# A Perceiver block on one core: in the blocks that project V, the previous head's value products between the two halves of the scores

## What is computed

```python
q = (layernorm(x) @ Wq + bq).reshape(B, L, NKV, G, HDIM)      # 8 kv heads, 4 query heads each
k, v = split(ctx @ Wkv + bkv)                                 # 6272 keys, 8 heads of 128
scores = einsum("blkgd,bmkd->bkglm", q, k) / sqrt(128)
attn = softmax(scores, axis=-1)
o = einsum("bkglm,bmkd->blkgd", attn, v)
x = x + o @ Wo + bo
...
w = NF4[codes] * scales          # 4-bit weights of the second part, expanded ahead of use
```

## Time and profile before

| | |
|---|---|
| median of 3 runs | 1162.08 us (1157.77 to 1168.44) |
| the profiled execution | 1156.21 us |
| its span, first to last instruction | 1154.40 us (mean granted TensorE clock 0.968) |
| block 0 starts, block 55 starts | 67.08 us, 1032.40 us |
| PE, DVE, POOL, ACT busy | 94%, 82%, 54%, 39% of the span |

### The profile page before, as it was taken

How to read it: one execution, slowest core, us unless ns; L and a number is a source line. 1 busy time by engine, 2 the same in 40 slices (tenths; PEclk the granted TensorE clock), 3 DMA queues, 4 the chain that set the end, 5 groups by cost and what they waited for, 6 DMA issues and landing times. The chain is left out here.

```text
span 1154.4 us, 23709 instructions
## 1 busy us (share of the span) xinstructions
PE 1079.8 (94%) x7035; PEld 954.4 (83%) x7035; DVE 945.8 (82%) x2331; ACT 444.6 (39%) x993; POOL 627.0 (54%) x1303
## 2 busy tenths in 40 slices
PE   6889999999999999899999999999999999995587
PEld 4889989899899989799899889998999999982132
DVE  3358998889988889888899888999898998884365
ACT  2134444344443444334443434444434443431030
POOL 2036675665666666656656666657666556652100
PEclk9689999999999999999999999999999999996879
DMA  9512121112212122121221221212221111114991
GB/s 358 201 38 70 57 63 59 60 53 71 59 47 72 55 61 62 53 59 51 65 63 51 64 65 50 70 41 62 72 63 49 56 43 51 47 46 161 337 379 55
DMA packets 66852, 99.26 MB, mean 86 GB/s; under 512 B 7780, under 2 KB 34916, under 8 KB 65956
## 3 DMA queue, kind: packets, MB, share of 16 engines
q1 hardware_dynamic: 63954, 86.97, 23.9%
q10 hardware_dynamic: 2178, 8.34, 2.1%
q0 software_dynamic: 592, 2.40, 0.6%
HBM read 82.79 MB, written 14.89 MB: 85 GB/s over the span
## 5 line engine op out<-in xcount | busy, mean ns | idle before, releaser
L439 POOL TENSOR_SCALAR leaf<-bit 128x256 f32<-128x256 uint16 x896 | 402.4, 449 | 113.0 <-DVE bit L776 29.1
L788 DVE COPY_PREDICATED leaf<-bit,leaf 128x256 f32<-128x256 uint16 x784 | 388.4, 541 | 50.4 <-POOL leaf L439 14.6
L461 POOL TENSOR_TENSOR leaf<-leaf,scale 128x256 f32<-128x256 f32 x112 | 81.2, 735 | 185.3 <-DVE leaf L788 184.4
L644 ACT ACTIVATE v_hi<-p_kv 128x256 fp32r<-128x256 f32 x196 | 75.2, 384 | 175.6 <-PE p_kv L61 175.5
L59 PE MATMUL p_kv<-wkv_hi,ctx_even_hi 128*128 128x256 f32 x448 | 128.1, 286 | 5.6 <-DVE v_lo L727 4.6
L644 ACT ACTIVATE k_hi<-p_kv,bk_sb 128x448 fp32r<-128x448 f32 x112 | 70.8, 632 | 156.6 <-PE p_kv L61 156.1
L739 DVE TENSOR_TENSOR pt_lo<-p_t,pt_hi 128x512 fp32r<-128x512 f32 x224 | 128.8, 611 | 1.6 <-ACT pt_hi L655 1.2
L655 ACT ACTIVATE pt_hi<-p_t 128x512 fp32r<-128x512 f32 x224 | 115.0, 542 | 33.9 <-PE p_t L544 33.8
L60 PE MATMUL p_kv<-wkv_lo,ctx_even_hi 128*128 128x256 f32 x448 | 125.9, 281 | 0.0
L61 PE MATMUL p_kv<-wkv_hi,ctx_even_lo 128*128 128x256 f32 x448 | 125.7, 281 | 0.0
L727 DVE TENSOR_TENSOR v_lo<-p_kv,v_hi 128x256 fp32r<-128x256 f32 x196 | 82.2, 419 | 46.0 <-ACT v_hi L644 45.6
(11 more groups left out here) (190 smaller groups left out, 2523.7 us busy)
## 6 DMA issues: line engine op xcount, KB each, us to landing
code<-in_codes SPq DMA_DIRECT2D x56, 256.0 KB, 2.6
scale<-in_scales SPq DMA_DIRECT2D x112, 128.0 KB, 3.0
expanded_weights<-leaf SPq DMA_DIRECT2D x112, 128.0 KB, 1.7
wring<-expanded_weights SPq DMA_DIRECT2D x28, 512.0 KB, 12.5
ctx_st<-in_ctx_t SPq DMA_DIRECT2D x96, 112.0 KB, 2.1
wq_sb<-in_wq SPq DMA_DIRECT2D x8, 1024.0 KB, 14.0
wring<-in_wo SPq DMA_DIRECT2D x16, 512.0 KB, 12.4
stage<-in_wkv ACTq DMA_DIRECT2D x4, 1024.0 KB, 8.6
```

The costliest lines, as they stand in the source:

```text
L439: m = nc.gpsimd.tensor_scalar(leaf[:, b, slot, :], bit0[:, b * HW:(b + 1) * HW], NF4[2 * j + 1] - NF4[2 * j], NF4[2 * j], ALU.mult, ALU.add)
L461: nc.gpsimd.tensor_tensor(leaf[:, b, 4, :], leaf[:, b, 0, :], scale[:, b * HW:(b + 1) * HW], ALU.mult).then_inc(scaled, 1)
L644: nc.scalar.activation(dst, src, ACT.Identity, bias=0.0 if bias is None else bias).then_inc(kv_rounded, 1)
L788: return nc.vector.copy_predicated(leaf[:, b, slot, :], bit[:, b * HW:(b + 1) * HW], leaf[:, b, other, :])
```

## The change

On PE, `scores` takes the list of halves that it is to compute. In even blocks the order becomes half 0 of the scores, `prev_values`, half 1 of the scores, `values`. Odd blocks stay as they are. On DVE, in even blocks, `add_output` of block i-2 and three takes of the weight expansion (`high_by_bit2(i-1, 0)` and the two of `high_by_bit1(i-1, 1)`) move from behind `score_stats` to between its two halves. No instruction is added or taken away, and no buffer changes.

```diff
-            def scores(i, h, kuse, static):
-                for c in range(2):
+            def scores(i, h, kuse, static, halves):
+                for c in halves:
                     pe.wait_ge(kv_split, kuse + c + 1)
...
-                scores(i, h, kuse, first)
-                if not first:
-                    prev_values(s, h)
                 if h % 2 == 0:
+                    scores(i, h, kuse, first, (0,))
+                    if not first:
+                        prev_values(s, h)
+                    scores(i, h, kuse, first, (1,))
                     values(s, h, half)
+                else:
+                    scores(i, h, kuse, first, (0, 1))
+                    if not first:
+                        prev_values(s, h)
...
-            def score_stats(i, h, half):
+            def score_stats(i, h, half, meanwhile=None):
                 now = 0 if half else 3
                 for c in range(2):
+                    if c == 1 and meanwhile:
+                        meanwhile()
                     for r in range(RT):
...
-                score_stats(i, h, half)
-                if not (first and h < 2):
+                def finish_previous():
+                    add_output(i - 2, (h - 2) % NKV)
+                    high_by_bit2(i - 1, 0)
+                    high_by_bit1(i - 1, 1)
+
+                score_stats(i, h, half, finish_previous if h % 2 == 0 and not (first and h == 0) else None)
+                if h % 2 == 1 and not (first and h < 2):
                     add_output(i - 2, (h - 2) % NKV)
                 if h % 2 == 0:
                     if not (first and h == 0):
-                        high_by_bit2(i - 1, 0)
-                        high_by_bit1(i - 1, 1)
                         high_by_bit2(i - 1, 1)
```

## The result

The changed kernel takes 1210.94 us (median of 4 runs, 1208.58 to 1219.25), the kernel before 1163.35 beside it: ratio 1.042, 95% interval 1.035 to 1.049. It is slower by 4.2%, where 1210 us was forecast. The profiled execution took 1210.41 us, its span 1208.6.

What follows compares the result with a forecast made beforehand. PE's order was taken to bound the kernel, DVE close behind. 17 x 1.95 + 9 x 1.72 + 0.98 = 49.7 us on the profiled 1156.21 made 1205.9, or 1211.8 by the median; 1210 was given, range 1190 to 1226.

Steps and rivals of the forecast that it cites:

- The wait for `pt_lo`: PE, even blocks, ahead of the value products: a new wait of 0.87 us, plus 0.10 restart, 0.97 in all.
- The wait ahead of V: PE, even blocks, half 1's score reads before V: a new wait of 0.88 us, plus 0.10 restart, 0.98 in all.
- The moved work on DVE: DVE, even blocks, between the score halves: addition and three takes cost nothing, DVE being free half a microsecond early.
- No catch-up: V's stalls (0.53, 0.28) and the odd block's 0.42 us come again unchanged, shifted with V: a gain of nothing.
- The 17 blocks: Even blocks like the one shown, paying both new waits: 1.95 us each, 33.2 us together.
- The 9: Even blocks where `pt_lo` ends 1.90 us after the block's start instead of 2.13: 1.72 us each, 15.5 together.
- The one behind the loop's turn: One even block where DVE has caught up, so only the second wait is paid: 0.98 us.
- The level: Base for the sum: profiled execution 1156.21 us gives 1205.9; the median, 5.9 above, gives 1211.8.
- Rival 1: DVE's catch-up shrinks the old stalls and pays part back: 20 us less, 1190 us; chance 0.11.
- rival 2: DVE sets the period, `pt_lo` ends 0.9 us earlier, no first wait: 15 us faster, about 1147; chance 0.03.
- Rival 3: Moved takes run at 0.73 us instead of 0.37, too late for half 1: 13 us more, 1223; chance 0.08.
- Rival 4: PE's clock falls to 1.2 GHz, twelve scores cost 2.0 us more, 27 times: 54 us, 1264; chance 0.04.

Runs made afterwards that it cites:

- The run with the tile's own wait: Changed kernel, but V's tile 0 waits only for the first score read of half 1, tile 1 for the second: 1200.86 us, ratio to before 1.037.
- the short takes: Takes cut to 8 of 256 columns, table values made small: kernel before 1114.08 us, ratio 0.959; changed kernel 1162.22 us, ratio 1.000.
- the two moved stalls: Two runs on the kernel before: odd blocks' value products split around half 1, 1158.98 us; `v_lo` of tile 4 made ahead of a take, 1162.30 us.

## Why the prediction was right

- **The wait for `pt_lo`** was put at 0.87 us; 0.84 was measured in the block shown, with the release at 0.05 (587.67 to 587.72) and the restart at 0.10 (587.72 to 587.94 instead of 0.12) as in rows 6.
- **The wait ahead of V** was put at 0.88 and measured at 0.88. Every piece of it came from before: the latency from a score matmul to its read, though seen only once, at the loop's turn, held.
- **The even block** was to grow by 1.95 us and grew by 24.58 - 22.72 = 1.86. The missing 0.09 is small change: `pt_lo` ended 2.08 us into this block (2.13 in the one of rows 4 and 5), and half 1's six starts span 591.36 - 590.33 = 1.03, not 1.06.
- **The moved work on DVE** cost nothing, as said, with 0.84 us to spare and not 0.5.
- **No catch-up.** The predicted zero was right: the odd block and V's inner stall came back unchanged. The reason given (everything hangs on V's start) was nearly right. The run with the tile's own wait shows that it hangs on the first `v_lo`, which follows V's start only as long as ACT is free.
- **The sum**, 49.7 us, met 49.5 us in the loop, partly by luck. The 17 blocks grew by 33.1 us, where 33.2 was forecast. The 9 grew by 16.3 and not 15.5. The one behind the loop's turn was to grow by 0.98 and became 0.26 shorter: it pays the second wait only, as said, but the granted clock stayed at 1.00 there, where the kernel before had 0.50. The odd blocks and the first one bring another 0.4. So the excess of the 9 and the gift of the clock cancel.
- **A cover that the prediction missed.** In three of the 9 blocks (the first of a chunk, inside the loop), the 0.05 us from `pt_lo` to the matmul did not hold. The block that the prediction names as its example, at 659.45 in the changed kernel, grew by 2.01 and not 1.72. DVE's row stands first, then PE's:

```profile
660.34 1.01 DVE L744 TENSOR_TENSOR pt_lo<-p_t,pt_hi 128x512 fp32r<-128x512 f32 x2
661.61 0.36 PE L59 MATMUL p_o<-pt_hi,v_hi 128*128 128x256 f32 x1 [0.71 <-DVE pt_lo L744]
```

  `pt_lo` ends at 661.35, and the products start 0.26 later. In these three blocks the trace has two more steps of PE's sequencer between the two, the waits of L578 (at 661.39) and L580 (at 661.50). In the kernel before, the same two stood at 631.74 and 631.84, under the matmuls of half 1. Three times 0.2 us make 0.6 of the 0.8 by which the 9 blocks exceed their forecast.
- **The count** of 17 and 9 blocks is borne out by the short takes: there the last `pt_lo` ends 1.91 us into each of the 26 blocks, and the loss is 46.1, near 27 x 1.72.
- **The level.** 1205.9 by the profiled execution and 1211.8 by the median; the changed kernel's profiled execution was 1210.4, of which 4.7 us are prologue and tail, not the change. That part of the agreement is luck of the clock in the prologue.
- **The rivals.** Rival 1 (part paid back) and rival 2 (DVE sets the period, not slower) fell, though DVE does set the length of the pairs in the kernel before: rival 2's picture of a DVE-bound kernel was right, as the short takes (4% faster) and the two moved stalls show. It fell on the point that it had named: `pt_lo` did not end 0.9 us earlier against the block's start, but at 2.08 us, where it had been 2.13. Rival 3 (late takes) fell: DVE was idle. Rival 4 (the clock) fell: the granted clock is 1.00 in the blocks shown, and at the loop's turn too, where it had dropped to 0.50 before. The Trainium skill, "TensorE: Matmul & The Clock Gate", section "A second HAM failure mode: psum-queue depth-cycling", says that short idles between groups of matmuls can make the clock swing. This trace does not show it: with two waits of 0.9 us in every 24.6 us the granted clock is 1.00 over the whole loop.

## What to carry to other kernels

Before an instruction group is moved on the engine that bounds the kernel, list what it stood in front of: it is the cover for every handover between the group before and the group behind. A handover that must go over another engine has a price that no free time on that engine lowers (here 2.1 us from the first matmul of the scores to the release by the reads, against 1.26 us of matmuls), and it can be added up from the trace of the old order. Look also at steps of the engine's own sequencer behind the wait: here they came into the open in three blocks. And where an engine at 80% busy time sets the pace through a chain, a stall on the bounding engine is only the place where the chain shows: cover it, and look for it at the next handover before counting it as won.

## What was not expected of the hardware

At the loop's turn PE stands still for as long after as before (2.8 us for issue), yet the granted clock fell to 0.50 there before and not in the changed kernel. PE's timeline and the stretch around it:

```profile
511.92 0.47 PE L59 MATMUL p_s<-k_hi,q_hi 128*128 128x448 f32 x1 [2.77 <-issue]
```

```profile
505.00:516.00 11.00, 8.23 (x57) 7.58 (x56) 8.25 (x21) 3.08 (x6) 4.76 (x11) 1.00 0.16 43
```

The same idle time can thus cost a piece at 1.2 GHz or not. Over the twelve kernels profiled here, PE stood still for 2.67 to 3.84 us at this place; in eight of them the granted clock fell to 0.50 around it, and in four it stayed at 1.00 (idle times of 2.77, 2.87, 2.94 and 3.26 us). It fell at 2.67 and at 2.82, so the length of the idle time alone does not decide; what does is not shown. The two blocks around the turn together are up to 1.0 us shorter or 2.3 us longer than in the kernel before. The prologue adds up to 3 us in the same way. Neither belongs to an edit: comparing the starts of blocks, and not spans, takes the prologue's part out, and leaving out the two blocks at the turn takes out the other.
